# Later clearing of segment cells, three places for the sheets' batches, and a smaller descriptor scratch in a fused GNN and expert kernel

## What is computed

```python
def _hconv(x, src, dst, ew, w1, b1, w2, b2, g, b):
    h = relu(x @ w1 + b1)
    msg = ew[:, None] * h[src]
    agg = segment_sum(msg, dst, num_segments=x.shape[0])
    h = agg @ w2 + b2
    return relu(_bn(h, g, b))

x = x + gnn(layernorm(x), edge_index, edge_weight, ...)   # two _hconv, with batch norms
x = x + ffn(layernorm(x), ...)                            # 8 experts, three matmuls each
```

## Time and profile before

| | us |
|---|---|
| median of three runs | 4843.56 |
| lowest and highest of them | 4843.49, 4847.84 |
| span of the profiled execution | 5228.2 |
| busy in it: PE, DVE, ACT, POOL | 4623.3, 2688.7, 2435.6, 2110.6 |
| first dense part | 0 to 174 |
| first aggregation | 174 to 1748, its last pieces to about 1798 |
| second dense part | to 1928 |
| second aggregation | 1928 to 3421 |
| norms and experts | to 5228 |

### The profile page before, as it was taken

One profiled execution on the slowest core, in us unless ns is written; L12 is line 12 of the kernel. 1 busy time (PEld: TensorE's weight loads), 2 busy tenths in 40 slices (PEclk: granted clock), 3 DMA queues, 4 the chain that ended last, 5 costly groups with the idle time before them and its releaser, 6 DMA issues. The chain is left out here.

```text
span 5228.2 us, 71544 instructions
## 1 busy us (share of the span) xinstructions
PE 4623.3 (88%) x25508; PEld 3800.6 (73%) x25508; DVE 2688.7 (51%) x6606; ACT 2435.6 (47%) x4218; POOL 2110.6 (40%) x2284
## 2 busy tenths in 40 slices
PE   6778888888999579888988988649999999999999
PEld 5667777666677467776666666548888888888888
DVE  7666666566333464522222222366666666666665
ACT  4655556666211263300000000057777777777777
POOL 1466666566666456666666666630000000000000
PEclk9889999999999789999999999779999999999999
DMA  5467777566755247876666666431111111001110
GB/s 155 148 210 271 243 240 245 188 211 217 236 198 201 77 141 268 277 243 218 218 219 205 226 212 224 131 96 25 30 28 33 33 33 33 24 26 33 33 28 15
DMA packets 546618, 770.23 MB, mean 147 GB/s; under 512 B 149720, under 2 KB 441411, under 8 KB 546262
## 3 DMA queue, kind: packets, MB, share of 16 engines
q1 hardware_dynamic: 328176, 382.01, 21.7%
q0 software_dynamic: 100944, 273.96, 16.4%
q10 hardware_dynamic: 117142, 109.65, 6.5%
HBM read 605.58 MB, written 147.26 MB: 144 GB/s over the span
## 5 line engine op out<-in xcount | busy, mean ns | idle before, releaser
L1106 PE MATMUL pf<-work 128*128 128x330 f32 (+4 forms) x3528 | 1251.9, 491 | 63.3 <-DMA work<-front 31.3
L1054 POOL DMA_INDIRECT wst<-h,src_col x1040 | 1000.3, 962 | 541.9 <-issue 275.0
L1106 PEld LDWEIGHTS pf<-work 128*128 128x128 f32 x3528 | 661.0, 197 | 402.2 <-issue 220.1
L2096 DVE TENSOR_TENSOR f_hl<-f_hf,f_hh 128x1024 fp32r<-128x1024 f32 (+1 forms) x400 | 479.7, 1199 | 636.3 <-ACT f_hf L1959 636.0
L1952 ACT ACTIVATE f_hh<-f_p,f_sh,f_sc 128x512 fp32r<-128x512 f32 (+1 forms) x800 | 571.7, 768 | 395.9 <-PE f_p L2194 394.5
L1273 ACT ACTIVATE ah<-agg 128x1024 fp32r<-128x1024 f32 (+1 forms) x50 | 51.8, 1037 | 1464.2 <-DVE agg L1420 1086.6
L1138 PEld LDWEIGHTS ps<-oh,wst 128*128 128x128 f32 x4160 | 543.4, 203 | 144.5 <-issue 99.6
L1138 PE MATMUL ps<-oh,wst 128*128 128x128 f32 x4160 | 560.7, 288 | 88.6 <-issue 55.1
L1054 POOL DMA_INDIRECT f_xr<-h,src_col x518 | 497.7, 961 | 282.8 <-issue 134.0
L1054 POOL DMA_INDIRECT f_u<-h,src_col x512 | 491.1, 959 | 260.5 <-issue 136.7
L1959 ACT ACTIVATE f_hf<-f_p,f_sh,f_sc 128x512 f32<-128x512 f32 (+1 forms) x800 | 572.5, 775 | 0.0
(11 more groups left out here) (285 smaller groups left out, 7648.0 us busy)
## 6 DMA issues: line engine op xcount, KB each, us to landing
work<-h SPq DMA_DIRECT2D x216, 512.0 KB
work<-front SPq DMA_DIRECT2D x50, 924.0 KB
front<-agg ACTq DMA_DIRECT2D x12, 3300.0 KB
work<-front SPq DMA_DIRECT2D x50, 756.0 KB
work<-front SPq DMA_DIRECT2D x50, 660.0 KB
work<-front SPq DMA_DIRECT2D x50, 580.0 KB
front<-agg ACTq DMA_DIRECT2D x8, 2600.0 KB
work<-front SPq DMA_DIRECT2D x25, 832.0 KB
```

What stands on the lines that cost most here:

```text
L1054: g.indirect_dma_start(G[t % R], None, h_dram[layer], bass.IndirectOffsetOnAxis(ap=src_col[:, col:col + 1], axis=0)).then_inc(ga[t % R], 16)
L1106: ins = g.matmul(pF[:, k, 0:count * w].rearrange("p (s c) -> p s c", c=w), HB[a % 2][0:r, n, k * P:(k + 1) * P], x, start=b == 0, stop=b = ...
L2096: g.tensor_tensor(hlo[l][q % 2][:, :, 0:nn], hf[l][:, :, 0:nn], hhi[l][q % 2][:, :, 0:nn].bitcast(fp32), ALU.subtract).then_inc(f_lo[l], 1)
```

## The change

Three edits. The clearing of a segment's cells begins behind the third group of the segment before it, no longer behind the second, and still ends with the segment's own first group at the latest. `work` has three places for batches, so batch a waits for batch a - 3. The descriptor scratch shrinks from its default of 16,384 bytes to 4,096 bytes per partition; the third place takes 9,376 bytes.

```diff
-        batch_in = [sem(f"batch_in{i}") for i in range(2)]
+        NBATCH = 3
+        batch_in = [sem(f"batch_in{i}") for i in range(NBATCH)]
...
-                work_w = max(2 * AB_W + 2 * HB_W, GT * TW + 2 * GW)
+                work_w = max(NBATCH * (AB_W + HB_W), GT * TW + 2 * GW)
...
-                            if a >= 2:
-                                g.wait_ge(f_mm, B0 + a - 1)
+                            if a >= NBATCH:
+                                g.wait_ge(f_mm, B0 + a - NBATCH + 1)
...
-                                g.wait_ge(batch_in[a % 2], batch_value(layer, a))
+                                g.wait_ge(batch_in[a % NBATCH], batch_value(layer, a))
...
-                                at = list(range(min(begun[m - 1] + 2, begun[m]), begun[m] + 1))[:CLEARS]
+                                at = list(range(min(begun[m - 1] + 3, begun[m]), begun[m] + 1))[:CLEARS]
...
-    nc = bacc.Bacc("TRN2", target_bir_lowering=False, num_devices=1)
+    nc = bacc.Bacc("TRN2", target_bir_lowering=False, num_devices=1, dynamic_dma_scratch_size=4096)
```

More of the change, by code:

```diff
@@ L773, in batch_value @@
         def batch_value(layer, a):
-            each = [[16 * (1 + len(batch_rows(x % NHG))) for x in range(a % 2, n, 2)] for n in NFL]
-            return layer * sum(each[0]) + sum(each[layer][:a // 2 + 1])
+            each = [[16 * (1 + len(batch_rows(x % NHG))) for x in range(a % NBATCH, n, NBATCH)] for n in NFL]
+            return layer * sum(each[0]) + sum(each[layer][:a // NBATCH + 1])
         SEG_SEQ = [[k for i in made for k in range(SHEET_S[i], SHEET_S[i + 1])] for made in MADE]
@@ L954, in aggregate @@
                 w2h, w2l = (sb(s, f"w2{layer}_{n}", [P, KC, C], f32r)[:, :, :] for n in ("hi", "lo"))
-                work_w = max(2 * AB_W + 2 * HB_W, GT * TW + 2 * GW)
+                work_w = max(NBATCH * (AB_W + HB_W), GT * TW + 2 * GW)
                 work = sb(s, f"work{layer}", [P, work_w])
-                AB = [work[:, i * AB_W:(i + 1) * AB_W] for i in range(2)]
-                HB = [work[:, 2 * AB_W + i * HB_W:2 * AB_W + (i + 1) * HB_W].rearrange("p (b n) -> p b n", n=C) for i in range(2)]
+                AB = [work[:, i * AB_W:(i + 1) * AB_W] for i in range(NBATCH)]
+                HB = [work[:, NBATCH * AB_W + i * HB_W:NBATCH * AB_W + (i + 1) * HB_W].rearrange("p (b n) -> p b n", n=C)
+                      for i in range(NBATCH)]
                 banks = [ps(s, f"ps{layer}_{i}", [P, CH]) for i in range(2)]
@@ L1022, in load @@
                                     g.wait_ge(hot_f[m % 2], hot_f_value(layer, m))
-                            if a >= 2:
-                                g.wait_ge(f_mm, B0 + a - 1)
+                            if a >= NBATCH:
+                                g.wait_ge(f_mm, B0 + a - NBATCH + 1)
                             for b, k, r in batch_rows(hg):
                                 lo = (hg * HG + b) * P
-                                g.dma_start(HB[a % 2][0:r, b:b + k, :],
-                                            h_dram[layer][lo:lo + k * r, :].rearrange("(k p) n -> p k n", p=r)).then_inc(batch_in[a % 2], 16)
-                            g.dma_start(AB[a % 2][:, 0:count * HG * w], front_dram[i][hg]).then_inc(batch_in[a % 2], 16)
+                                g.dma_start(HB[a % NBATCH][0:r, b:b + k, :],
+                                            h_dram[layer][lo:lo + k * r, :].rearrange("(k p) n -> p k n", p=r)).then_inc(batch_in[a % NBATCH], 16)
+                            g.dma_start(AB[a % NBATCH][:, 0:count * HG * w], front_dram[i][hg]).then_inc(batch_in[a % NBATCH], 16)
                         for n in range(NF):
@@ L1100, in unit @@
                             if n == 0:
-                                g.wait_ge(batch_in[a % 2], batch_value(layer, a))
+                                g.wait_ge(batch_in[a % NBATCH], batch_value(layer, a))
                                 if hg == 0 and p >= 1:
                                     g.wait_ge(f_add, added_segs(layer, p - 1))
-                            x = AB[a % 2][0:r, 0:count * HG * w].rearrange("p (s b c) -> p s b c", b=HG, c=w)[:, :, n, :]
+                            x = AB[a % NBATCH][0:r, 0:count * HG * w].rearrange("p (s b c) -> p s b c", b=HG, c=w)[:, :, n, :]
                             for k in range(KC):
                                 ins = g.matmul(pF[:, k, 0:count * w].rearrange("p (s c) -> p s c", c=w),
-                                               HB[a % 2][0:r, n, k * P:(k + 1) * P], x, start=b == 0, stop=b == NB - 1)
+                                               HB[a % NBATCH][0:r, n, k * P:(k + 1) * P], x, start=b == 0, stop=b == NB - 1)
                             if b == min((hg + 1) * HG, NB) - 1:
```

## The result

| | before | after |
|---|---|---|
| median of the runs beside each other, us | 4844.77 (4 runs) | 4795.67 (4 runs, 4791.49 to 4800.84) |
| ratio, with its 95% interval | | 0.9896 [0.9882, 0.9909] |
| profiled execution: own time, span, us | not given, 5228.2 | 4800.84, 4799.0 |

The change makes the kernel 49 us faster, 1.0%. The forecast was 14.5 us.

The account below looks back on a forecast made before the run. The prediction took PE and POOL, waiting for each other in turns in the two aggregations, as the bound. Terms -13.5 + 2 - 3 + 0 + 0 = -14.5 us off 4843.6 gave 4829 us, range 4795 to 4862.

Parts of the forecast that it names:

- Three places: PE's waits for batches, nearly all in the second aggregation, go with a third place in `work`: -13.5 us, bounds 0 and -43.
- The load at the start: One more batch load, issued without a wait at each aggregation's start, delays the first product: +2 us, bounds 0 and +5.
- Later clearing: ACT's waits for stores before clearing, 32.5 us in 11 places, go: -3 us, bounds 0 and -10.
- The wider last piece: DVE's first add of a segment waits for a larger last clearing piece: 0 within slack, up to 29 us without.
- A scratch of 4 KB: POOL's gathers need no waits for room in the smaller descriptor scratch: 0, bounds 0 and 67 us.
- More than the profile shows: Rival, 0.10: batches late more often in timed runs; PE's 43.0 us of batch waits and 2.9 for lows come off: 4798.
- Hidden anyway: Rival, 0.27: POOL's pace decides in the timed runs and PE's waits fall into its slack: 4843 us.
- The last clearing is late: Rival, 0.10: in faster timed runs DVE stands at the first add of 20 segments, price 29 us: 4861.
- the scratch is too small: Rival, 0.08: POOL makes room once per 16 gathers, 67 us, of which 50 land on the path: 4879.

Follow-up runs that it names:

- the second profile: The kernel before, unchanged, run and profiled once more: 4844.96 us, ratio 0.9999 against the kernel before, profiled span 4852.2 us.

## Why the prediction was right and wrong

**What bounds the kernel.** The prediction had PE and POOL waiting for each other in turns, and 1.254 us a gather; both stand. It had 518 - 385 = 133 us of POOL's waits left in the timed runs, and the second profile shows 118. But it drew the wrong inference from them, that POOL's pace may then hide more. It hides less. In the last 160 gathers of the second aggregation, where no edit's wait stands, four gathers took 5.82 us on average in the first profile, with 35 us of waits in all put down to "remote"; in the second profile they take 5.05 us and POOL doesn't wait once. So the slack that PE's waits could fall into is a part of the slow level. In the timed runs the two chains above show a loss by PE passing on to POOL nearly whole. The step that failed is that the sum "is made in the profile's waits and taken off the median as it is", which the prediction called the weak step: the two terms of gain came to 16.5 us, and the runs show 29.5 and 26.5.

**Three places, -13.5 us; measured -29.5 alone, with the scratch.** The mechanism was right, as shown by the waits (29.4 to 6.4 us, all but one gone). Mis-sized was the share that passes on. I took three tenths of the shorter waits from one at 2808 that fell into a slack of 2.02 us which only the slow level has. At the timed level they pass on, as from 1.93 to 3.86 us at 2026, and bring more with them: in the second aggregation 21.0 us of waits went, PE is busy 1221.98 - 1212.23 = 9.8 us less without them, 30.8 in all, and the stretch is 26 us shorter.

I had set aside the Trainium skill's rule ("TensorE: Matmul & The Clock Gate", on how the clock's oscillation bites in real kernels), that the product behind a DMA wait starts at the low clock, because "short waits leave the product behind them near its usual length". That is wrong for most waits of 1.7 us and more: the products at 1926.87 and 2027.70 above show it, and the granted clock of 0.50 behind the first of them agrees with the page, which tells it of longer waits than most of these. It doesn't hold of each wait: behind the one of 2.44 us the clock is 1.00. The gain by that sentence, 20 us more than 14.5, would have been 34.5 in place of the forecast; for this part alone it would have been 33.5, against 29.5.

**The load at the start, +2 us; measured about 1.** From SP's first load in the first aggregation, PE's first piece starts 6.26 us later before (345.67 to 351.93) and 7.38 with the change (346.71 to 354.09), 1.1 us more; the wait ahead of it is 4.49 and 6.39. At the start of the second, the first product comes 6.18 us behind the first gather before and 6.65 with the change, but 6.14 in its second profile, and 5.57 to 6.63 in the other builds with two places: no cost can be told there.

**Later clearing, -3 us; measured -26.5.** The largest error, and outside its bounds (0 to -10). Two steps failed. The waits were taken from the slow level, 32.5 us, where 125.0 stand in the timed one. And the price was read from "PE's wait for lows shows only once": that view goes by named releasers, and 19.3 of PE's 24.7 us of waits for lows, the 4.48 at 563.54 among them, are put down to "issue". That "the store has had the time of one more group" and the waits go was right: 17.4 us are left. **The wider last piece, 0,** was right in the sum: in the changed profile DVE waits for ACT's clearing 0.8 us in 2 places, against 4.6 in 2 before. But the claim that 2 us of slack are left was wrong at the timed level: those two places are the first adds of segments 3 and 4 (273.97 and 303.76), which start 0.14 us behind the end of the clearing after waits of 0.65 and 0.17 us, so no slack is left there. No run on the first level showed what one group later would cost. **A scratch of 4 KB, 0,** was right to within the 3.8 us: at the first level a gather takes 0.963 us on average with 16 KB and 0.965 with 4 KB.
**The rivals.** *More than the profile shows* (0.10, 4798) is where it landed, 4795.67, though by another sum: it took off 43.0 us of waits for batches and 2.9 for lows, where the runs show 29.5 and 26.5 from two edits, and batches were not late more often (29.4 us in 17 places by the same view that showed 31.3 in 15). So its nearness is luck, and so is that the measured time lies inside the range, 0.7 us above its lower end, which was that rival's. *Hidden anyway* (0.27) gives the time of the second level, the one that its rows were read from; whether POOL's pace is what hides the waits there was not tried. *The last clearing is late* and *the scratch is too small* did not happen.

**A wrong number ahead of the prediction.** The kernel's description says that `work` holds 2 x (1320 + 1024) floats, and the change's that the third place takes 9,376 bytes. The widest sheet's part has 7 segments, 7 x 4 x 66 = 1848 floats, so it is 2 x (1848 + 1024), and the third place takes 2872 x 4 = 11,488 bytes of the 12,288 that the scratch gives up. No term rested on it. It also counts the groups one too low: `begun[m - 1]` is the segment's first group, so before the change the clearing begins behind the third group (`+ 2`), and with it behind the fourth or, in a segment of three groups, behind the next segment's own first.

## What to carry to other kernels

Compare the span of a profiled execution with the median before any term is made from its waits: where they differ by 8% as here, the waits and slacks of that profile are not those of the timed runs. Here small stalls that fell into slack in it passed on in the timed runs, and stalls that it showed with 32.5 us were worth as much as any. Count the floor of the engine that issues ahead (gathers times pace, 2070 x 1.254 = 2596 us, against 2718 us of stretches in the second profile), and ask of each wait whether it is part of the 122 us by which the stretches are longer than that floor. A helper engine that stands at a wait for work that is not urgent, clearing for a later segment, with urgent work queued behind it, costs a part of each of its waits (here a quarter to a half), even where the view of waits doesn't name it at the engine that bounds. Where a wait is put down to "issue", compare its end with the ends of what the code waits for there.

## What the runs showed of the hardware

- The same program took 4845 us in three sittings and 5221 to 5256 in three others. In the profiled executions of the second level the first dense part (some 175 us) and the experts (1809 to 1812) are as long as on the first, and each aggregation of the kernel before and of the change is 170 to 215 us longer. Two sittings at different levels were reported with the same chip number, so it may not be a property of a chip.
- In the second aggregation a wait of PE of 1.7 to 2.7 us lengthened the 16 records of the next gathered product from 1.95 us to 2.30 to 3.20 in five of seven places, where 1.5 us and less left it at 1.95. Right behind the wait of 2.73 us the granted clock was 0.50.
- A descriptor scratch of 2 KB in place of 16 KB cost nothing that could be told (1.0002 [0.9993, 1.0011]) with up to 16 gathers outstanding at the first level, and at the second the kernel was 0.5% slower with it (1.0054 [1.0040, 1.0069]). In both its gathers' records were the longest in sum: 2007.0 us against 1993.9 to 1999.1, and 2015.0 against 1985.6 to 1994.5. With 4 KB they were as with 16.
